# Row maxima of a score step: one reduction over two banks instead of one per bank

## The reference

```
xn = layernorm(x)
h  = layernorm(xn) * g1 + b1
q, k, v = heads(h @ WQ + bQ), heads(h @ WK + bK), heads(h @ WV + bV)   # 16 heads of 8
scores  = q k^T / sqrt(8), only keys with 0 <= i - j < 128, else -inf
attn    = softmax(scores)                  # needs the maximum of each row and head
ao      = attn @ v ;  attn_out = ao @ WO + bO
ssm     = scan(s = A*s + h @ Bw) @ Cw ;  g = sigmoid(h @ Wg + bg)
x1      = xn + g*attn_out + (1-g)*ssm
s       = x1 + gelu(layernorm(x1) @ W1 + b1) @ W2 + b2
f       = top-2-of-8 expert MLP of rmsnorm(xn), added to xn
out     = x + s * silu(f)
```

## Time and profile before

| | us |
|---|---|
| median of three runs | 1007.69 |
| the three runs | 1007.69, 1010.56, 1004.4 |
| profiled execution | 1014.14 |
| its span, first to last instruction | 1012.4 |
| mean granted TensorE clock | 0.962 of full speed |

### The profile page before, as it was taken

How to read it: one execution, slowest core, us unless ns; L and a number is a source line. 1 busy time by engine, 2 the same in 40 slices (tenths; PEclk the granted TensorE clock), 3 DMA queues, 4 the chain that set the end, 5 groups by cost and what they waited for, 6 DMA issues and landing times.

```text
span 1012.4 us, 37892 instructions
## 1 busy us (share of the span) xinstructions
PE 873.0 (86%) x15768; PEld 544.5 (54%) x15768; DVE 725.8 (72%) x1749; ACT 740.7 (73%) x1302; POOL 498.6 (49%) x786
## 2 busy tenths in 40 slices
PE   4668989989898898989889898988989898898886
PEld 2344646556465565646556464555656455564635
DVE  7666877768687776878777686876768787676525
ACT  4437877868687787878778686877878787676855
POOL 6426273544736355473635537363563836434351
PEclk9659999999999999999999999999999999999979
DMA  6932334160242515124251512425142242510000
GB/s 146 206 68 84 49 113 68 50 128 20 97 68 81 100 49 122 26 97 67 81 99 50 121 28 97 68 81 99 48 108 31 97 68 70 100 36 10 7 22 11
DMA packets 85596, 75.14 MB, mean 74 GB/s; under 512 B 9457, under 2 KB 79154, under 8 KB 85426
## 3 DMA queue, kind: packets, MB, share of 16 engines
q1 hardware_dynamic: 83346, 71.93, 31.8%
q10 hardware_dynamic: 2080, 0.79, 0.3%
HBM read 36.26 MB, written 30.15 MB: 66 GB/s over the span
## 4 chain that ended last, share of the span: by engine, by line
PE 47%; DVE 24%; issue 14%; ACT 10%; POOL 3%; DMA 1%; SPq 1%; DVEq 0%; POOLq 0%; ACTq 0%
PE ps L568 6%; PE ps L775 6%; PE ps L825 5%; PE ps L510 5%; PE ps L786 5%; DVE mx L1187 5%; PE ps L499 3%; DVE gc L1299 3%; DVE lin L1292 2%; PE ps L769 2%; PE ps L587 2%; PE ps L582 2%; ACT pt L983 2%; PE ps L713 2%; PE ps L525 2%
## 5 line engine op out<-in xcount | busy, mean ns | idle before, releaser
L1187 DVE TENSOR_REDUCE mx<-ps 128x2 f32<-128x320 f32 (+1 forms) x512 | 223.2, 467 | 115.0 <-PE ps L525 113.3
L983 ACT ACTIVATE pt<-ps 128x1024 f32<-128x1024 f32 (+1 forms) x256 | 234.4, 918 | 96.7 <-PE ps L499 94.3
L1444 POOL TENSOR_SCALAR_AFFINE_SELECT pt<-pt 128x512 f32<-128x512 f32 x256 | 164.6, 645 | 228.5 <-ACT pt L983 226.0
L510 PE MATMUL ps<-kd,qz 48*32 48x160 bf16 (+1 forms) x4096 | 151.2, 239 | 47.3 <-DVE mx L1187 38.0
L499 PE MATMUL ps<-qz,kd 51*32 51x256 bf16 (+1 forms) x4096 | 165.0, 268 | 1.8 <-ACT pt L983 1.0
L568 PE MATMUL ps<-pt,va 128*32 128x256 f32 (+1 forms) x2048 | 154.2, 380 | 8.3 <-POOL pt L1447 5.1
L510 PEld LDWEIGHTS ps<-kd,qz 48*32 48x32 bf16 x4096 | 75.8, 92 | 157.3 <-issue 59.1
L775 PEld LDWEIGHTS ps<-m,act_t 128*128 128x128 f32 x1024 | 126.8, 191 | 51.7 <-DVE act_t L1320 36.7
L775 PE MATMUL ps<-m,act_t 128*128 128x128 f32 x1024 | 143.2, 283 | 8.8 <-DVE act_t L1320 8.3
L1447 POOL TENSOR_SCALAR_AFFINE_SELECT pt<-pt 128x512 f32<-128x512 f32 x192 | 129.7, 675 | 0.0
L1025 ACT ACTIVATE lin<-ps,mbias 128x512 f32<-128x512 f32 x128 | 87.9, 686 | 47.1 <-DVE act_t L1320 29.3
(11 more groups left out here) (185 smaller groups left out, 1612.8 us busy)
## 6 DMA issues: line engine op xcount, KB each, us to landing
qz<-qk_parts SPq DMA_DIRECT2D x32, 384.0 KB, 6.3
kd<-qk_parts SPq DMA_DIRECT2D x32, 384.0 KB, 9.8
qk_parts<-qp SPq DMA_DIRECT2D x16, 384.0 KB, 2.6
qk_parts<-kp SPq DMA_DIRECT2D x16, 384.0 KB, 2.4
xl<-L_attn_x SPq DMA_DIRECT2D x16, 256.0 KB, 3.3
qk_parts<-qp SPq DMA_DIRECT2D x16, 256.0 KB, 3.0
qk_parts<-kp SPq DMA_DIRECT2D x16, 256.0 KB, 2.8
xnr<-xn SPq DMA_DIRECT2D x16, 256.0 KB, 3.9
```

The source lines that it names most:

```text
L510: nc.tensor.matmul(ps[QG * c:QG * (c + 1), 4 + par, w * pr:w * (pr + 1)], qz[q][rows, 2 * g + pr, P * i + QG * c:P * i + QG * (c + 1)], kd ...
L983: nc.scalar.activation(to, src, ACT.Exp, scale=SCALE).then_inc(exp_ok.sem, 1)
L1187: nc.vector.tensor_reduce(mx[:, i, HG * g + pr:HG * (g + 1):2], src, AX.X, ALU.max).then_inc(mx_ok.sem, 1)
L1444: sel1 = nc.gpsimd.affine_select(out=pt[:, s, :, 0:P], in_=pt[:, s, :, 0:P], compare_op=ALU.is_ge, fill=0.0, base=0, pattern=[[0, HG], [1, ...
```

## The change

One function, `maxima(m, n)`, takes the place of `maximum(m, n, pr)`. It waits for both halves of the step and reduces banks 4 and 5 with one instruction, four heads into four columns of mx. mx_ok counts 16 for a batch instead of 32, and both halves of PE's step n wait for the same value, that all n steps before are reduced. In DVE's loop it stands at pr = 0 in front of the other work of both half steps. The number of elements reduced and the results are the same.

```diff
-        mx_ok = signal("mx_ok", 2 * NCH)
+        mx_ok = signal("mx_ok", NCH)
...
-                        pe.wait_ge(*done(mx_ok, b + 1, 2 * n - 1 + half))
+                        pe.wait_ge(*done(mx_ok, b + 1, n))
...
-            def maximum(m, n, pr):
+            def maxima(m, n):
                 g, i = n // NT, n % NT
                 w = WIN if i else P
-                dve.wait_ge(*done(s_ps, m, 2 * n + pr + 1))
+                dve.wait_ge(*done(s_ps, m, 2 * n + 2))
                 if n == 0:
                     dve.wait_ge(*done(nm_step, m - 1))
-                src = bank(4 + pr)[:, 0:2 * w].rearrange("p (r k) -> p r k", r=2)
-                nc.vector.tensor_reduce(mx[:, i, HG * g + pr:HG * (g + 1):2], src, AX.X, ALU.max).then_inc(mx_ok.sem, 1)
+                src = ps[:, 4:6, 0:2 * w].rearrange("p c (r k) -> p c r k", r=2)
+                to = mx[:, i, HG * g:HG * (g + 1)].rearrange("p (r c) -> p c r", c=2)
+                nc.vector.tensor_reduce(to, src, AX.X, ALU.max).then_inc(mx_ok.sem, 1)
...
                 for n in range(NCH):
-                    maximum(0, n, 0)
-                    maximum(0, n, 1)
+                    maxima(0, n)
...
-                        if nxt and n < NCH:
-                            maximum(b + 1, n, pr)
+                        if nxt and n < NCH and pr == 0:
+                            maxima(b + 1, n)
```

## The result

The changed kernel takes 1049.12 us (median of four runs, 1047.91 to 1054.92), the kernel before 1009.12 us on the same chip: ratio 1.041, interval 1.035 to 1.047. It is slower by 40 us. The prediction said slower by 29.3 us (1037), with a range of 1020 to 1052. The profiled execution took 1048.52 us with a span of 1046.8, against 1014.14 and 1012.4: +34.4.

The account below looks back on a forecast made before the run. It took PE and DVE, waiting for each other in a ring of scores and maxima, as the bound. 15 passes x 1.6 = 24 us plus 5.3 us of prologue, +29.3 on 1007.7, gave 1037 us, range 1020 to 1052.

Parts of the forecast that it names:

- direction: Whole kernel: slower, chance 0.91, against 0.05 for faster and 0.04 for the same.
- mechanism: PE and DVE turns: the first bank is released only by the joint maximum, which must wait for the second half's mask.
- the single prices: Joint reduction on DVE: 0.82 us for 640 elements, 0.69 for 512, about 0.07 us shorter than the pair.
- the 15 to 25 of the forecast: DVE's busy time over the whole run: down some 15 to 25 us.
- the ring in a free turn, 13 to 14 (e): Loop turn without other DVE work between maxima: 1.67 us mask to mask instead of 1.20; +0.46, sum +1.41.
- the walk through a pass: Last masks of the loop's turns followed one by one: nearly nothing net at turn 8, then losses up to +1.62 us.
- (c) to (f): Turn 10 to last exp: +0.81 us carried to turn 12, then sums +0.95 at 13, +1.41 at 14, +1.62 at 15.
- the rival of slack: Gaps in the loop absorb the carried delay; only the last two turns and prologue count: +15 us, 1023; chance 0.10.
- the prologue: Batch 0's score pass before the loop: turns of 1.54 us instead of 1.16, fourteen of them, +5.3 us, none hidden.
- so I charge nothing: TensorE's clock: PE's added idle of some 1.6 us a pass is small, prologue already at the lower level; no cost.

Follow-up runs that it names:

- two_after: behind, but the next turn's first half also waits for the second maximum, so both banks are released late; 1030.10 us, ratio 1.0206.
- late_start: behind, but the first maximum waits for both halves' masks, banks still released one by one; 1022.46 us, ratio 1.0111.
- prologue_only: Kernel before with the joint maximum only in batch 0's pass ahead of the loop; 1016.31 us against 1009.79, ratio 1.0063.
- loop_only: Kernel before with the joint maximum only in the loop's 15 passes, two reductions a turn in the prologue; 1041.47 us, ratio 1.0326.
- behind: Kernel before, two reductions each with its own bank's release, but DVE operations that stood between them moved behind the second; 1004.14 us, ratio 0.996.
- half_len: Changed kernel with the joint maximum over only half of each head's columns, same waits and releases; 1002.28 us, ratio 0.9943.
- joint_some: Joint maximum only at loop turns 1, 2, 3, 5, 6 and 7, pairs elsewhere as in the kernel before; 1021.63 us, ratio 1.012.
- filler2: filler with the wait for the exp stated again behind the repeated matmuls, so two waits precede the turn's matmul; 1049.92 us, ratio 1.0389.
- filler: Changed kernel plus repeated score matmuls in PE's idle time at seven turns, ahead of the wait for the maximum; 1038.84 us, ratio 1.0274.
- joint_swap: Changed kernel with PE's two waits before a turn exchanged, maximum first, exp second; 1025.20 us, ratio 1.0174.
- behind_early: behind with PE's wait for the exp moved ahead of the values of the turn before; 984.55 us, ratio 0.9762.
- behind_swap: behind with PE's wait for the exp put behind its wait for the maximum; 983.03 us, ratio 0.9745.

## Why the prediction came out as it did

**Right: direction, mechanism and the single prices.** The joint reduction saves next to nothing: 0.82 and 0.69 us forecast, 0.823 and 0.687 measured. The cost row of the Trainium skill ("VectorE: DVE Perf Modes", the section on the trn2 errata) gives 0.79 us, so the trace is 4% above it; and its advice for chained operations (the same page, Rules for kernel authors: "Don't try to fuse for perf — DRAIN happens regardless. Minimize op *count*, not sems"), which I took to speak for this change, holds no gain here: the operations became fewer and the time longer, because the instruction that goes was also the one that freed a bank half a microsecond early. DVE's busy time fell by 35 us, more than the 15 to 25 of the forecast: 21 in the maxima (223.2 to 201.9), the rest mainly in three small operations (cmb from 0.98 to 0.60 us each, cr from 0.52 to 0.19, mr from 0.56 to 0.23). What they met before and don't meet now, I haven't followed.

**Right: the ring in a free turn, 13 to 14 (e).** 1.69 us against 1.67. two_after and late_start show its two causes apart.

**Right: the walk through a pass, once undisturbed passes are compared.** The last mask of a turn came later than before by the times below. The second row is pass 7, the third is pass 8 of the changed kernel (565.02 to 625.18, its second shortest, with no such pause and full clock) against the same undisturbed pass 7 of the kernel before.

```text
turn        2     3     4     5     6     7     8     9    10    12    13    14   exp 15
forecast  -0.1   0.0  +0.2  +0.4  +0.2  +0.2 -0.15 +0.36 +0.81 +0.81 +0.95 +1.41 +1.62
pass 7   -0.12 +0.10 +0.28 +0.28 +0.25 +0.21 +0.30 +0.35 +0.82 +1.44 +1.61 +2.10 +2.28
pass 8   -0.12 +0.10 +0.28 +0.28 +0.10 +0.06 -0.21 +0.21 +0.68 +0.75 +0.92 +1.40 +1.59
```

In the undisturbed pass every entry is within 0.15 us of the forecast, and the losses (c) to (f) came as they were added up: +0.07 from turn 10 to turn 12, +0.17 to 13, +0.48 to 14, +0.19 to the last exp. So the rival of slack is refuted too: the delay of turn 10 is carried to turn 12. Of the +1.59 at the last exp, 0.08 came back before the next pass, hence the +1.51. Pass 7 left this line at two places, shown by the next rows, of turn 8 and of project_v at turn 10:

```profile
518.44 0.24 PE L510 MATMUL ps<-kd,qz 48*32 48x128 bf16 x4 [0.51 <-DVE mx L1188]
518.68 0.58 PE L510 MATMUL ps<-kd,qz 48*32 48x128 bf16 x4
...
525.12 1.05 PE L620 MATMUL ps<-wv,hT 128*128 128x128 f32 x7 [0.86 <-issue]
```

Four score matmuls take 0.24 us, the next four, equal ones, 0.58; and project_v stands 0.86 us behind nothing that the profile shows.

**Slightly low: the prologue.** 1.62 us a turn, not 1.54: from the masks' end to the DVE's start it is 0.13, not the 0.06 that I took. The turns sum to 5.8 us for my 5.3; prologue_only measured 6.5.

**The term that was mis-sized: "so I charge nothing".** The forecast put no price on TensorE's clock, nor on anything else that disturbs the ring. By its undisturbed parts the change costs 15 x 1.51 + 7.8 = 30.5 us (with the pause in its prologue); the measured 40 have some 10 more.

What the pauses are can be read from the traces. DMA queue q8 carries packets of kind "instruction", 16 KB each, 125 in the run of the changed kernel, and each comes ahead of a fixed place in PE's program (here about 125 matmuls apart). The longest pause of the changed kernel:

```profile
828.45 0.26 PE L525 MATMUL ps<-edge,identb 64*32 64x128 bf16 x1 [2.03 <-issue]
```

```profile
q8 instruction: 1, 0.02, 36.2%
```

The second row is the queue in the window from 825.8 to 826.0 us: this packet started at 825.89 and landed at 827.05, and PE went on 1.40 us behind it. The 14 traces hold 103 pauses of PE over 0.45 us that the profile puts down to "issue" from the first score on (some in the middle of equal matmuls, some between groups), and every one of them ends 1.2 to 1.7 us behind the landing of such a packet. The 0.58 us row above does too (1.33 us). The places also recur: the matmul that goes on at 828.45 is the same one in the loop_only, two_after, late_start, behind and half_len traces. So PE stood waiting for its own instructions. In behind, the median transfer starts with 82 matmuls to go before the place where it is needed; the five longest waits follow transfers that started with 28 or fewer. Why a transfer starts late isn't settled.

What such waits and the half clock cost can be read pass by pass. Of the 196 periods (14 in each of the 14 profiled executions), 94 have neither: they stand 0.03 us above the shortest of their kernel in the median, at most 0.8. The other 102 stand 1.2 us above it, and hold 93% of all the time above the shortest. A fit over all periods gives 0.86 us for each us of waiting for instructions and 0.32 us for each us at half clock, and accounts for 94% of the variance.

The table sets this beside the measured differences. "Clean" is 15 times the change of the shortest period plus the change of the prologue, in us against the kernel before; "measured" is between the medians; "rest" is measured less clean; "waits" are those for instructions in the loop of the profiled execution, in us; "half clock" is the time as above. "Fit" is an estimate of the rest from the last two columns at the two rates, with the prologue, which is at half clock in all of them, left out.

```text
kernel          shortest  clean  measured  rest  fit   waits  half clock
before            58.64      0        0      0    0      4.1      68
prologue_only     58.59     +7       +7      0   -3      3.5      69
loop_only         60.07    +22      +32     +9  +10      7.2      92
after             60.16    +30      +40    +10  +10      7.6      96
joint_some        58.55     -1      +13    +14   +8      5.4      89
filler2           60.27    +33      +41     +8   +5      7.3      82
two_after         58.96    +11      +20    +10   +8     12.4      75
late_start        58.73     +9      +13     +4   +4     11.3      66
behind            57.48    -17       -6    +12  +11     17.7      66
half_len          57.13    -20       -7    +14   +6     13.7      62
filler            59.54    +23      +30     +7   -1      3.9      75
joint_swap        59.31    +18      +17     -1   -3      0.0      76
behind_early      57.25    -21      -25     -4   -7      2.2      49
behind_swap       57.16    -22      -26     -4   -8      1.1      51
```

Two things can be read from it. The nine kernels with a rest of 4 us or more all have more waits or more half clock than the kernel before: loop_only, after and joint_some mainly the clock, behind and half_len the waits. And the three in which the wait for the exp no longer stands in front of the binding one have few waits and no rest. That goes with the misses of size in the experiments: behind_swap gains 5 us over behind by its shortest period and 16 by the rest. The fit is within 4 us in ten of the thirteen and falls 6 to 8 us short in joint_some, half_len and filler.

It is association, not proof: no kernel moved the waits or the clock alone, and filler2 has a higher clock than the changed kernel and no less time. The rest is also partly a matter of which executions are compared: between the two profiled ones it is 4 us and not 10 (+34.4 against 30.5), since the profiled one of the kernel before was itself 5 us above its median. Why a slower ring spends more time at half clock, and why the order of two waits changes the waits for instructions, stays open.

## What to carry to other kernels

When two engines pass banks back and forth, a second instruction on the second bank isn't overhead: it is what lets one engine refill a bank while the other reads the next. Merging saves the fixed part (here 0.07 us a pair) and costs the overlap (here half a microsecond a turn), so price the turn, not the instruction. Before an experiment on such a ring, look at the waits in front of its first instruction and put the one that is met last first, or state the early one earlier: here that was worth 2% (21 us over behind), of which a quarter lies in the undisturbed periods and the rest came with fewer waits for instructions and less half clock. And look at the passes one by one: compare undisturbed ones with undisturbed ones before a step of a forecast is called wrong.

## What the runs showed that I had not expected

- Two waits in front of PE's first score matmul cost by their order. With the wait for the exp (long met) first and the binding one second, PE starts 0.15 us behind the maximum; with the binding one first, or alone, mostly 0.05 us. filler and filler2 show it in both directions, and joint_swap at every turn where the maximum binds; in some turns of behind_swap and behind_early it is 0.12 to 0.14.
- An idle time called "issue" can be a wait: the exchange of two waits turned 70.5 us of "issue" into 14.6, and 7.9 us of waits for the maximum into 101.3. And a releaser named by the profile can be a coincidence: 45.7 us on an exp that PE didn't wait for.
- A reduction over two banks in one instruction costs by its elements, as over one bank: 0.49 us for 320 elements over two banks, 0.823 for 640.
- PE can stand still for want of its own instructions. Such pauses, 0.46 to 3.5 us each, make up 1 to 18 us of a run, depending on the kernel, and end 1.2 to 1.7 us behind the landing of a 16 KB packet on the instruction queue. The profile calls them "issue". The one in the prologue after follows a packet that landed at 53.42:

```profile
54.83 0.31 PE L510 MATMUL ps<-kd,qz 48*32 48x160 bf16 x2 [1.65 <-issue]
```
